# A one-core transformer layer with routed experts: the last three tiles' sums made on chip by TensorE, and the requests for rows moved in the transition

## The chip, the cores and the metric

The kernel runs on one core of one Trainium2 chip. The metric is device time in microseconds (us); lower is better. A core has five engines that run their own instruction queues and wait for each other by semaphores: TensorE (PE, with its weight loads PEld), VectorE (DVE), ScalarE (ACT), GpSimd (POOL) and SyncE (SP), which here only issues DMAs. POOL issues the indirect DMAs (scatter of rows, accumulation of rows in DRAM). All DMAs share 16 DMA engines.

## What is computed

```python
x = x + _layernorm(attention(_layernorm(x)))          # 4 x 256 tokens of 256, 16 heads of 128, rotary, causal
x = x + _layernorm(moe(_layernorm(x)))                # below
logits = x @ router_weight.T + router_bias            # 16 experts
top_val, top_idx = jax.lax.top_k(logits, 4)           # each token goes to 4 experts
gate_up = einsum('th,ehd->etd', x, gate_up_proj) + gate_up_proj_bias
glu = gate * sigmoid(1.702 * gate)                    # gate, up clipped at 7
out = einsum('etd,edh->eth', (up + 1.0) * glu, down_proj) + down_proj_bias
out = (out * router_scores.T[:, :, None]).sum(axis=0) # sum over a token's 4 experts
```

All data is float32.

## The kernel before

**Attention** runs over 64 slots (4 batches x 16 heads) and fills the first two thirds of the time. **Routing** follows batch by batch (`choose`, `share`, `place` on DVE; `ranks`, `counts` on PE): every token's normalised row, its expert weights and its token number (column TOKEN) are scattered by POOL to `rows_d` in DRAM, 4 times (once for each chosen expert), so that the rows of one expert stand together. 8 scatters belong to the last batch.

**The tiles.** The rows are then worked in TILE_MAX = 47 tiles of 128 rows, each of one expert. For tile i: SP loads its rows to `xg` (`load_rows`, 9 buffers; which rows, a table in SBUF says, and SP reads it first); PE turns them (`turn_tile`, into `xgT` by ACT), multiplies by the expert's weights, which DVE and ACT have copied to `gu_now` (`place_gu`, one half each; PE: `gate_up`); DVE clamps (`clamp`), ACT applies the gelu, DVE multiplies (`gated`); PE multiplies by the second weights (`down`); ACT scales by the router weight (`weigh`, to `y`); POOL adds the 128 rows of `y` to their tokens' rows in DRAM by an indirect DMA with addition (`add_rows`). There are SUMS = 3 arrays in DRAM, `sum0` to `sum2`, and tile i goes to array i % 3, so that additions to one array are never in flight together. `sum0` starts with the second bias term (`start_sum`, from `start_sums` on PE and `start_out` on ACT).

Tiles 0 to EARLY - 1 = 8 hold full tiles of the first three batches, known from `early_table` before the last batch is routed. They are worked while the last batch is routed; I call this stretch (about 331 to 380 us) the transition. Tiles 9 to 46 come from `table`, which needs all counts: PE `counts`, DVE `plan_tiles`, PE `table_rows`, DVE `table_out` (semaphore dve_table).

In the steady loop, PE's order in turn i is `turn_tile(i + 1)`, `gate_up(i)`, `down(i - 2)`; DVE's is `place_gu(i + 1)`, `clamp(i)`, `gated(i)`; ACT's is `place_gu(i + 1)`, `xgT_out(i + 1)`, `gelu(i)`, `weigh(i - 2)`. The order is written out by hand, for the transition call by call.

**The end.** When all additions have landed, SP loads the three arrays in 12 DMAs; for each quarter u (two of the eight groups of 128 tokens) DVE adds the three arrays and takes mean and variance, POOL computes 1/sqrt(var + eps) (`power`), ACT normalises, DVE adds `x`, and SP stores the quarter.

```python
for i in range(SUMS):
    sp.wait_ge(dma_sum[i], 16 * ((TILE_MAX - 1 - i) // SUMS + 1))
```

## Time and profile before

| | before |
|---|---|
| median of 3 runs | 517.08 us (516.77 to 518.73) |
| time of the profiled execution | 519.65 us |
| its span, first to last instruction | 517.8 us |
| busy: PE, PEld, DVE, ACT, POOL | 460.6, 430.1, 357.0, 327.3, 243.7 us |
| mean granted TensorE clock | 0.965 of full speed |

The span is what the trace shows; the profiled execution took 1.85 us more than its span. Busy shares are means over the whole kernel: PE is busy for 89% of the span, but not in the last 30 us. TensorE's clock is granted at one of two levels, 2.4 GHz (1.00) and 1.2 GHz (0.50).

### The profile page before, as it was taken

To read this page: it belongs to the slowest core of one execution; us is meant where nothing else is said; L and a number is where in the kernel's file an instruction comes from. 1 tells how busy PE (TensorE), PEld (TensorE's weight loads), DVE (VectorE), ACT (ScalarE), POOL (GpSimd) and SP (SyncE) were. 2 spreads that over 40 slices of the span, in tenths; PEclk is the share of its full clock that TensorE was granted. 3 is DMA by queue.
4 is the path that set the end of the run, shared out by engine and by line. 5 is a ranking of instruction groups with operands and counts; after the bars stand their busy time and mean duration, and the time that the engine had idled before them with its cause. 6 is when DMAs were issued, how large, how long until landed. Compare 5 with 4: busy or idle time off the path is not lost. (4 is left out here: it accounts for less than half of the span.)

```text
span 517.8 us, 11511 instructions
## 1 busy us (share of the span) xinstructions
PE 460.6 (89%) x3402; PEld 430.1 (83%) x3402; DVE 357.0 (69%) x1254; ACT 327.3 (63%) x815; POOL 243.7 (47%) x230
## 2 busy tenths in 40 slices
PE   7698999999999999999999999788799999999600
PEld 4698898999899999899999988677599999999500
DVE  4798787686865686865686896276557776767435
ACT  4778987767576767576767565555446565656602
POOL 1888874354122265343552145036625555555612
PEclk9999999999999999999999999898989999999955
DMA  7367552999300000000464455523545565655482
GB/s 238 108 204 245 179 184 66 373 369 370 112 1 1 22 25 35 35 13 35 174 219 123 151 199 186 161 61 90 107 92 97 100 103 95 102 95 87 52 243 92
DMA packets 63900, 67.86 MB, mean 131 GB/s; under 512 B 4640, under 2 KB 58720, under 8 KB 63840
## 3 DMA queue, kind: packets, MB, share of 16 engines
q1 hardware_dynamic: 54960, 55.79, 34.0%
q0 software_dynamic: 8304, 10.88, 12.8%
q8 instruction: 29, 0.48, 0.4%
q10 hardware_dynamic: 576, 0.46, 0.3%
q14 instruction: 31, 0.25, 0.2%
HBM read 32.63 MB, written 34.49 MB: 130 GB/s over the span
## 5 line engine op out<-in xcount | busy, mean ns | idle before, releaser
L494 POOL TENSOR_TENSOR by_sin<-by_sin,rope_sin 128x512 f32<-128x512 f32 x64 | 82.5, 1289 | 149.3 <-ACT by_sin L615 149.3
L590 POOL DMA_INDIRECT sum_d<-y,xg x47 | 72.9, 1551 | 64.5 <-ACT y L739 61.5
L615 ACT ACTIVATE by_sin<-bank 64x512 f32<-64x512 f32 x128 | 75.8, 592 | 33.9 <-PE bank L1246 32.5
L1444 PE MATMUL bank<-xgT,gu_now 128*128 128x128 f32 x752 | 94.0, 280 | 3.6 <-ACT xgT L615 2.7
L1444 PEld LDWEIGHTS bank<-xgT,gu_now 128*128 128x128 f32 x752 | 89.7, 196 | 4.6 <-issue 4.6
L637 ACT ACTIVATE prob<-score,row_bias 128x128 f32<-128x128 f32 (+1 forms) x128 | 57.1, 447 | 46.0 <-DVE row_bias L913 46.0
L1246 PE MATMUL bank<-xT_h,qk_h 128*128 128x256 f32 x256 | 77.6, 303 | 4.3 <-DVE qkT L903 1.7
L913 DVE CUSTOM_DVE_ANT_0 score<-bank,mask 128x128 f32<-128x128 f32 (+1 forms) x128 | 40.2, 351 | 52.1 <-issue 52.1
L1246 PE MATMUL bank<-xT_h,qk_l 128*128 128x256 f32 x256 | 72.3, 282 | 0.0
L1246 PE MATMUL bank<-xT_l,qk_h 128*128 128x256 f32 x256 | 72.2, 282 | 0.0
L1246 PEld LDWEIGHTS bank<-xT_h,qk_h 128*128 128x128 f32 x256 | 48.8, 191 | 5.1 <-POOL qk_l L479 3.4
L1456 PE MATMUL bank<-dn_w,act 128*128 x188 | 49.4, 388 | 1.1 <-DVE act L1111 1.0
L1246 PE MATMUL bank<-wo_h,oT_h 128*128 128x256 f32 x128 | 42.0, 328 | 9.3 <-DVE oT_l L928 9.1
L903 DVE TENSOR_TENSOR qkT<-bank,by_sin 128x512 f32<-128x512 f32 x64 | 44.2, 691 | 7.1 <-POOL by_sin L494 1.3
L1246 PEld LDWEIGHTS bank<-xT_l,qk_h 128*128 128x128 f32 x256 | 48.8, 191 | 0.0
L1246 PEld LDWEIGHTS bank<-xT_h,qk_l 128*128 128x128 f32 x256 | 48.7, 190 | 0.0
L1246 PE MATMUL bank<-wv_h,xT_h 128*128 128x256 f32 x128 | 47.5, 371 | 0.0
L895 DVE TENSOR_TENSOR bank<-bank,rope_cos 128x512 f32<-128x512 f32 x64 | 44.4, 694 | 1.2 <-ACT by_sin L615 1.2
L725 ACT ACTIVATE glu<-gate 128x256 f32<-128x256 f32 x47 | 19.6, 416 | 37.7 <-DVE gate L1095 37.7
L1095 DVE TENSOR_SCALAR gate<-bank,gate_bias 128x128 f32<-128x128 f32 x94 | 28.5, 345 | 20.6 <-PE bank L1444 20.4
L922 DVE TENSOR_SCALAR prob<-prob,row_rec 128x128 f32<-128x128 f32 (+1 forms) x128 | 40.3, 357 | 2.3
L615 ACT ACTIVATE gu_now<-gu_w 128x512 f32 x47 | 31.9, 678 | 15.8 <-issue 14.6
(171 smaller groups left out, 1141.0 us busy)
## 6 DMA issues: line engine op xcount, KB each, us to landing
rows_d<-blank SPq DMA_DIRECT2D x32, 576.0 KB, 7.4
gu_w<-_L_ffn_gate_up_proj_dram SPq DMA_DIRECT2D x16, 512.0 KB, 5.6
xg<-rows_d SPq DMA_DIRECT2D x47, 144.0 KB, 2.6
dn_w<-in_L_ffn_down_proj_dram SPq DMA_DIRECT2D x16, 256.0 KB, 3.0
sum_d<-blank SPq DMA_DIRECT2D x2, 1152.0 KB, 9.9
raw_qk<-in_L_attn_wq_dram SPq DMA_DIRECT2D x16, 128.0 KB, 3.6
raw_qk<-in_L_attn_wk_dram SPq DMA_DIRECT2D x16, 128.0 KB, 3.7
raw_v<-in_L_attn_wv_dram SPq DMA_DIRECT2D x8, 256.0 KB, 2.7
```

Of the source, the lines that this page charges most:

```text
L494: pool.tensor_tensor(v, v, rope_sin[:, :].unsqueeze(1).broadcast_to([P, 2, T]), ALU.mult).then_inc(pool_sin, 1)
L590: pool.indirect_dma_start(out=sum_d[i % SUMS], out_offset=bass.IndirectOffsetOnAxis(ap=xg[:, i % XG, TOKEN:TOKEN + 1].bitcast(U32), axis=0 ...
L615: return sc.activation(out, in_, ACT.Copy)
L637: e = sc.activation(prob[:, n % 2, lo:hi], score[:, n % 2, lo:hi], ACT.Exp, bias=row_bias[:, n % 2, i:i + 1], scale=-1.0, accum_out=row_su ...
L895: dve.tensor_tensor(v, v, rope_cos[:, :].unsqueeze(1).broadcast_to([P, 2, T]), ALU.mult).then_inc(dve_cos, 1)
L903: dve.tensor_tensor(qkT[:, n % QR, :, :].rearrange("p w t -> p (w t)"), ps_qk[n % 2][:, :], by_sin[:, n % 2, :], ALU.add).then_inc(dve_rop ...
L913: m = dve.tensor_tensor_reduce(score[:, n % 2, lo:hi], ps_s[:, lo:hi], mask[:, P:T] if i == 0 else mask[:, :], -1.0 / D, FILL, ALU.add, AL ...
L922: m = dve.tensor_scalar(prob[:, n % 2, lo:hi], prob[:, n % 2, lo:hi], row_rec[:, n % 2, i:i + 1], None, ALU.mult)
L1095: m = dve.tensor_scalar(gate[:, i % 2, r, :], ps_gu[i % 2][:, r * P:(r + 1) * P], gate_bias[:, bass.ds(e * 2 + r, 1)], LIMIT, ALU.add, ALU ...
L1246: m = pe.matmul(out, lhs, rhs, start=first and i == 0, stop=last and i == len(terms) - 1, skip_group_check=not (first and last))
L1444: m = pe.matmul(ps_gu[i % 2][:, (2 * s + r) * P:(2 * s + r + 1) * P], gu_now[:, i % 2, k, s, r * P:(r + 1) * P], xgT[:, i % XT, k, :], sta ...
L1456: m = pe.matmul(ps_y[i % 2][:, 0:M], act[:, i % AR, r, :], dn_w[:, bass.ds(e, 1), r, :].rearrange("p o m -> p (o m)"), start=(r == 0), sto ...
```

## The change

It has two parts, and small moves that go with them.

**The end.** The last LATE = 3 tiles (44 to 46) are no longer added in DRAM. ACT writes their weighted rows to `late_h` (rounded to the matmul's short float format) and DVE the rest to `late_l` (`late_low`). For each of these tiles DVE makes a 0/1 matrix `turn` (128 rows x 1024 tokens) from the token numbers (`rows_to_tokens`, in the turns of tiles 40, 41 and 42), and PE multiplies it with the rows, which puts them at their tokens (`add_late`, in PSUM). Since the arrays in DRAM are final after tile 43, SP loads them while the last tiles are worked: `sum2` after tile 41, `sum0` after 42, `sum1` after 43. POOL adds the three (`add_second`, `add_third`), and PE adds the result in PSUM by a product with the identity (`add_sums`). DVE takes the statistics from PSUM, `finish` multiplies and adds `x`, ACT adds the shift. `shift_x`, which ACT did at the end, goes into the turns of tiles 13 to 16.

**The transition.** SP asks for three tiles' rows before it stores the start of `sum0`; on PE, ACT and DVE several calls change place; POOL adds tile 2 after the 8 scatters instead of before.

```diff
@@ SP @@
-            start_sum(3)
             sp.wait_ge(dve_table, 1)
             sp.wait_ge(dma_scatter, 16 * TILES * TOP)
-            for i in range(EARLY, TILE_MAX):
+            for i in range(EARLY, EARLY + 3):
+                load_rows(i)
+            start_sum(3)
+            for i in range(EARLY + 3, TILE_MAX):
                 load_rows(i)
-
-            for i in range(SUMS):
-                sp.wait_ge(dma_sum[i], 16 * ((TILE_MAX - 1 - i) // SUMS + 1))
+            for i, to, signal in ((ENDING[0], sum_a, dma_first), (ENDING[1], sum_b, dma_second)):
+                sp.wait_ge(dma_sum[i], 16 * ((LAST - 1 - i) // SUMS + 1))
+                for u in range(2):
+                    sp.dma_start(to[:, 4 * u:4 * u + 4, :], sum_rows[i][:, 4 * u:4 * u + 4, :]).then_inc(signal[u], 16)
+            sp.wait_ge(dma_sum[ENDING[2]], 16 * ((LAST - 1 - ENDING[2]) // SUMS + 1))
             for u in range(4):
+                sp.dma_start(sum_c[:, 2 * u:2 * u + 2, :], sum_rows[ENDING[2]][:, 2 * u:2 * u + 2, :]).then_inc(dma_third[u], 16)
@@ POOL @@
-            for i in range(3):
+            for i in range(2):
                 add_rows(i)
             may_scatter(B - 1)
...
-            for i in range(EARLY, TILE_MAX):
+            for i in range(EARLY, LAST):
                 add_rows(i)
             for u in range(4):
+                add_second(u)
+            add_third(0)
+            add_third(1)
+            add_third(2)
+            power("moe", 0)
+            add_third(3)
@@ ACT @@
             gelu(1)
             normalise("b", B - 1, xn, x)
+            gelu(2)
+            moeT_out(B - 1)
             weigh(0, experts[0])
-            moeT_out(B - 1)
             weigh(1, experts[1])
-            gelu(2)
             gelu(3)
             load_table(ACT.Exp, 1)
             place_tile(4)
-            weigh(2, experts[2])
             expo_out(B - 1)
             load_table(ACT.Gelu_apprx_sigmoid, 2)
+            weigh(2, experts[2])
@@ DVE @@
             clamp(0, experts[0])
+            attn_stats(B - 1)
             experts[2] = place_gu(2)
-            attn_stats(B - 1)
...
             experts[7] = place_gu(7)
+            table_out()
             clamp(6, experts[6])
             gated(6)
             experts[8] = place_gu(8)
-            table_out()
...
+            def rows_to_tokens(j):
+                i = LAST + j
+                dve.wait_ge(dma_xg[i % XG], 16 * (i // XG + 1))
+                chain(dve.tensor_copy(token[:, j:j + 1], xg[:, i % XG, TOKEN:TOKEN + 1].bitcast(I32)))
+                chain(dve.tensor_scalar(from_end[:, j, :], full_edge[:, :], token[:, j:j + 1], None, ALU.subtract))
+                dve.tensor_tensor(turn[:, j, :, :], from_end[:, j, :].unsqueeze(2).broadcast_to([P, TILES, P]),
+                                  countdown[:, :].unsqueeze(1).broadcast_to([P, TILES, P]), ALU.is_equal).then_inc(dve_turn, 1)
             for i in range(EARLY, TILE_MAX):
...
                 gated(i)
+                if LAST - 4 <= i < LAST - 4 + LATE:
+                    rows_to_tokens(i - LAST + 4)
+            for j in range(LATE):
+                late_low(j, experts[LAST + j])
@@ PE @@
             down(2)
+            turn_tile(5)
             counts()
...
+            turn_tile(7)
             gate_up(6)
+            table_rows()
             down(5)
-            table_rows()
             start_sums(B - 1)
-            turn_tile(7)
+            turn_tile(8)
             gate_up(7)
...
+            def add_late(u, j, first=False, last=False):
+                pe.wait_ge(dve_turn, j + 1)
+                pe.wait_ge(dve_late, j + 1)
+                for s in range(2):
+                    for rows in (late_h, late_l):
+                        m = pe.matmul(ps_sum[u][:, s * M:(s + 1) * M], turn[:, j, 2 * u + s, :], rows[:, j, :], ...)
+            def add_sums(u):
+                pe.wait_ge(pool_whole, u + 1)
+                for s in range(2):
+                    pe.matmul(ps_sum[u][:, s * M:(s + 1) * M], ident[:, :], sum_a[:, 2 * u + s, :], start=False, stop=False, ...)
+            for u in range(4):
+                add_late(u, 0, first=True)
+            for u in range(4):
+                add_late(u, 1)
+                add_sums(u)
+                add_late(u, 2, last=True).then_inc(pe_sum, 1)
```

On SP, behind the last early tile's load, there stood (L376 stores the start of `sum0`, `started`; L428 reads the table, L431 loads rows):

```order
L431 DMA xg<-rows_d 128x288
L376 DMA sum_d<-started 128x2x256 [waits act_start]
L428 TENSOR_LOAD table [waits dma_scatter,dve_table]
L428 ISA x2
L431 ISA [waits dma_sum0]
```

Now the same queue goes on without the store (L393 there), which comes three loads later:

```order
L448 DMA xg<-rows_d 128x288
L445 TENSOR_LOAD table [waits dma_scatter,dve_table]
L445 ISA x2
L448 ISA [waits dma_sum0]
L448 DMA xg<-rows_d 128x288
L445 TENSOR_LOAD table
L445 ISA x2
L448 ISA [waits dma_sum1]
L448 DMA xg<-rows_d 128x288
L445 TENSOR_LOAD table
L445 ISA x2
L448 ISA [waits dma_sum2]
```

So the first request for tile 9's rows no longer stands behind a wait for ACT's `start_out` (act_start).

On PE, around `gate_up(6)` of the transition, there stood (L1444 `gate_up`, L1456 `down`, L1422 `table_rows`, L1411 `start_sums`, L1431 `turn_tile`):

```order
L1444 MATMUL bank<-xgT,gu_now 128x128 x7
L1451 TENSOR_LOAD early_table
L1451 ISA x2
L1456 ISA [waits act_y,dve_act]
L1456 MATMUL bank<-dn_w,act 128x256
L1456 ISA
L1456 MATMUL bank<-dn_w,act 128x256
L1422 MATMUL bank<-ident,plan 1x128 [waits dve_plan]
L1422 MATMUL bank<-ident,plan 1x128
L1411 MATMUL bank<-dnb,routeT 128x256 [waits act_routeT]
L1411 MATMUL bank<-dnb,routeT 128x256
L1431 MATMUL bank<-ident,xg 128x128 [waits act_xgT,dma_xg7]
```

Now there stands (L1509 `turn_tile`, L1522 `gate_up`, L1500 `table_rows`, L1536 `down`):

```order
L1509 MATMUL bank<-ident,xg 128x128 [waits act_xgT,dma_xg7]
L1509 MATMUL bank<-ident,xg 128x128
L1522 MATMUL bank<-xgT,gu_now 128x128 [waits act_xgT,dve_up,act_gu,dve_gu]
L1522 MATMUL bank<-xgT,gu_now 128x128 x7
L1500 MATMUL bank<-ident,plan 1x128 [waits dve_plan]
L1500 MATMUL bank<-ident,plan 1x128
L1529 TENSOR_LOAD early_table
L1529 ISA x2
L1536 ISA [waits act_y,dve_act]
L1536 MATMUL bank<-dn_w,act 128x256
```

The turn of tile 7 stands ahead of `gate_up(6)` instead of right before `gate_up(7)`, so that ACT can copy it while PE multiplies; tiles 5, 6 and 8 move in the same way. `table_rows` stands ahead of `down(5)`.

On DVE, in the turns of tiles 40, 41 and 42, three rows are new behind `gated` (L1169), ahead of the next `place_gu` (L1140, L1143):

```order
L1169 SCALAR_TENSOR_TENSOR act<-up,glu 128x256 [waits pe_y,dve_up,act_glu]
L1277 CAST token<-xg 128x1 [waits dma_xg8]
L1278 TENSOR_SCALAR from_end<-full_edge,token 128x8 [waits dve_stat]
L1279 TENSOR_TENSOR turn<-from_end,countdown 128x1024 [waits dve_stat]
L1140 TENSOR_LOAD table
L1140 ISA x2
L1143 ISA [waits pe_gu]
L1143 COPY gu_now<-gu_w 128x512
```

Before, `place_gu` followed at once. PE's next `gate_up` waits for that copy (dve_gu).

## Rows read from the trace of the kernel before

**Rows 1.** The chain that ended last, in order of time: start, us, what

```profile
490.58 3.74 DMA sum_d<-y,xg
...
495.32 4.16 DMA sum_c<-sum_d
...
506.82 0.75 DVE stats L876 x2
...
510.08 0.75 DVE stats L876 x2
...
511.16 0.17 DVE var_eps L883
...
513.21 0.85 DVE sum_b L1226 x2
```

**Rows 2.** Busy time in stretches of the end: PE, PEld, DVE, ACT, POOL, clock, DMA

```profile
488.00:494.00 6.00, 0.08 (x1) 0.00 (x0) 0.00 (x0) 3.66 (x9) 3.52 (x3) 0.83 0.57 66
500.00:505.00 5.00, 0.00 (x0) 0.00 (x0) 4.79 (x17) 1.09 (x2) 1.41 (x3) 0.50 1.05 345
```

**Rows 3.** Timeline of the transition: start, us, engine, line, instruction, idle before

```profile
348.37 0.18 DVE L966 TENSOR_TENSOR logits<-bank,rb 128x32 f32<-128x32 f32 x1
...
362.84 0.96 POOL L497 DMA_INDIRECT rows_d<-xrow,slot_of  x1 [0.30 <-issue]
...
367.71 0.40 DVE L1065 CAST table<-bank 1x256 int32<-1x256 f32 x1
...
371.78 5.50 SPq L431 DMA_DIRECT2D xg<-rows_d  x5
...
376.18 0.69 PE L1431 MATMUL bank<-ident,xg 128*128 128x128 f32 x2 [1.78 <-DMA xg<-rows_d]
...
379.94 1.95 PE L1444 MATMUL bank<-xgT,gu_now 128*128 128x128 f32 x16
```

**Rows 4.** Time from issue to landing of the last batch's eight scatters

```profile
DMA to landing us min/median/max: 2.4/2.5/3.5
```

**Rows 5.** Busy time in one stretch of the transition, columns as in rows 2

```profile
375.90:379.30 3.40, 3.12 (x15) 3.12 (x16) 0.34 (x1) 0.38 (x1) 0.00 (x0) 0.50 0.83 176
```

**Rows 6.** Timeline of the steady loop, one turn, in part

```profile
475.88 0.43 DVE L1085 COPY gu_now<-gu_w 128x512 f32 x1 [0.34 <-issue]
476.78 0.61 DVE L1095 TENSOR_SCALAR gate<-bank,gate_bias 128x128 f32<-128x128 f32 x2 [0.46 <-PE bank L1444]
477.42 0.42 ACT L725 ACTIVATE glu<-gate 128x256 f32<-128x256 f32 x1 [0.72 <-DVE gate L1095]
477.55 0.72 PE L1444 MATMUL bank<-xgT,gu_now 128*128 128x128 f32 x5
```

**Rows 7.** Groups by form: busy us, mean ns of one, idle before

```profile
L494 POOL TENSOR_TENSOR by_sin<-by_sin,rope_sin 128x512 f32<-128x512 f32 x64 | 82.5, 1289 | 149.3 <-ACT by_sin L615 149.3
L903 DVE TENSOR_TENSOR qkT<-bank,by_sin 128x512 f32<-128x512 f32 x64 | 44.2, 691 | 7.1 <-POOL by_sin L494 1.3 <-issue 0.4
L928 DVE TENSOR_TENSOR oT_l<-bank,oT_h 128x256 fp32r<-128x256 f32 x64 | 27.2, 425 | 18.9 <-ACT oT_h L615 18.8
L1074 DVE TENSOR_TENSOR wv_l<-raw_v,wv_h 128x512 fp32r<-128x512 f32 x1 | 1.8, 1791 | 0.0
```

**Rows 8.** Timeline of PE: pace of short-format products and of float32 products

```profile
204.22 0.28 PE L1246 MATMUL bank<-wo_h,oT_h 128*128 128x256 f32 x1
204.34 0.28 PE L1246 MATMUL bank<-wo_l,oT_h 128*128 128x256 f32 x1
...
353.57 1.49 PE L1456 MATMUL bank<-dn_w,act 128*128 x3
```

**Rows 9.** Additions in DRAM near the end: issues on POOL, and their time to landing

```profile
478.47 1.55 POOL L590 DMA_INDIRECT sum_d<-y,xg  x1 [1.32 <-ACT y L739]
...
484.40 1.56 POOL L590 DMA_INDIRECT sum_d<-y,xg  x1 [1.50 <-ACT y L739]
...
DMA to landing us min/median/max: 3.6/3.8/4.8
```

More of the change, by code:

```diff
@@ L41 @@
 BLANK = E * REGION
-XG, XT, AR, YR, SUMS = 9, 2, 3, 5, 3
+XG, XT, AR, YR, SUMS, LATE = 9, 2, 3, 5, 3, 3
 FILL_STEP = 4
@@ L175, in block_kernel @@
         sum_c = sb("sum_c", [P, TILES, M])
+        turn = sb("turn", [P, LATE, TILES, P], F32R)
+        late_h = sb("late_h", [P, LATE, M], F32R)
+        late_l = sb("late_l", [P, LATE, M], F32R)
+        token = sb("token", [P, LATE])
+        from_end = sb("from_end", [P, LATE, TILES])
         rows_d = nc.dram_tensor("rows_d", (BLANK + P, ROW), F32).ap()
@@ L214, in block_kernel @@
         dma_sum = [sem(f"dma_sum{i}") for i in range(SUMS)]
-        dma_result = [sem(f"dma_result{u}") for u in range(4)]
+        dma_first = [sem(f"dma_first{u}") for u in range(2)]
+        dma_second = [sem(f"dma_second{u}") for u in range(2)]
+        dma_third = [sem(f"dma_third{u}") for u in range(4)]
+        dve_turn = sem("dve_turn")
+        dve_late = sem("dve_late")
+        pool_first = sem("pool_first")
+        pool_whole = sem("pool_whole")
+        pe_sum = sem("pe_sum")
         dma_out = sem("dma_out")
@@ L329, in v_split @@
                 eng.wait_ge(pool_v, g + 1 - DVE_PAIRS)
+        LAST = TILE_MAX - LATE
+        ENDING = [(LAST + k) % SUMS for k in range(SUMS)]
         def entry(i, column):
@@ L602, in _, with add_second, add_third @@
                     scatter(t, k)
-            for i in range(3, EARLY):
+            for i in range(2, EARLY):
                 add_rows(i)
             pool.wait_ge(dma_start, 16 * B)
-            for i in range(EARLY, TILE_MAX):
+            for i in range(EARLY, LAST):
                 add_rows(i)
-            for u in range(4):
+            def add_second(u):
+                pool.wait_ge(dma_first[u // 2], 16)
+                pool.wait_ge(dma_second[u // 2], 16)
+                tiles = slice(2 * u, 2 * u + 2)
+                pool.tensor_tensor(sum_a[:, tiles, :], sum_a[:, tiles, :], sum_b[:, tiles, :], ALU.add).then_inc(pool_first, 1)
+            def add_third(u):
+                pool.wait_ge(dma_third[u], 16)
+                pool.wait_ge(pool_first, u + 1)
+                tiles = slice(2 * u, 2 * u + 2)
+                pool.tensor_tensor(sum_a[:, tiles, :], sum_a[:, tiles, :], sum_c[:, tiles, :], ALU.add).then_inc(pool_whole, 1)
+            for u in range(4):
+                add_second(u)
[4 more added lines that the diff above has]
+            add_third(3)
+            for u in range(1, 4):
                 power("moe", u)
@@ L736, in weigh @@
                 sc.wait_ge(pe_y, i + 1)
+                if i >= LAST:
+                    sc.activation(late_h[:, i - LAST, :], ps_y[i % 2][:, 0:M], ACT.Copy,
+                                  scale=xg[:, i % XG, bass.ds(e + M, 1)]).then_inc(act_y, 1)
+                    return
                 if i >= YR:
@@ L852, in _, with shift_result @@
                     weigh(i - 2, experts[i - 2])
+                if EARLY + 4 <= i < EARLY + 8:
+                    shift_x(i - EARLY - 4)
+            def shift_result(u):
+                n = NORMS.index(("moe", u))
+                sc.wait_ge(pool_shift, n + 1)
+                sc.wait_ge(dve_out, u + 1)
+                for i in range(2):
+                    sc.activation(sum_b[:, 2 * u + i, :], sum_b[:, 2 * u + i, :], ACT.Identity,
+                                  bias=shift[:, 2 * n + i:2 * n + i + 1]).then_inc(act_moe, 1)
             for u in range(4):
-                shift_x(u)
-            for u in range(4):
-                normalise("moe", u, sum_a, sum_a, act_moe)
+                shift_result(u)
         @block.vector
@@ L1454, in down @@
                     pe.wait_ge(act_y, i - 1)
+                if i - 2 >= LAST:
+                    pe.wait_ge(dve_late, i - 1 - LAST)
                 for r in range(2):
@@ L1558, in _ @@
                     down(i - 2)
+            def add_late(u, j, first=False, last=False):
[3 more added lines that the diff above has]
+                    for rows in (late_h, late_l):
+                        m = pe.matmul(ps_sum[u][:, s * M:(s + 1) * M], turn[:, j, 2 * u + s, :], rows[:, j, :],
+                                      start=first and s == 0 and rows is late_h, stop=last and s == 1 and rows is late_l,
+                                      skip_group_check=True)
+                return m
+            def add_sums(u):
+                pe.wait_ge(pool_whole, u + 1)
+                for s in range(2):
+                    pe.matmul(ps_sum[u][:, s * M:(s + 1) * M], ident[:, :], sum_a[:, 2 * u + s, :], start=False, stop=False,
+                              skip_group_check=True)
+            pe.wait_ge(act_xgT, TILE_MAX)
+            for u in range(4):
[4 more added lines that the diff above has]
+                add_late(u, 2, last=True).then_inc(pe_sum, 1)
 _INS = ["L0_attn_x", "L0_attn_wq", "L0_attn_wk", "L0_attn_wv", "L0_attn_wo", "L0_ffn_router_weight", "L0_ffn_router_bias",
```

44 lines of the change are left out of this document (24 added, 20 removed).

## The prediction

> **What bounds the kernel now.** I read the chain that ended last first, since it says where an earlier step gives an earlier end. From 490.58 us on it holds no PE work at all: the last addition in DRAM (3.74 us), the loads of the three arrays (the first DVE step of the end waits for a DMA issued at 495.32 that takes 4.16 us), then DVE, quarter by quarter, and the last store [rows 1]. Two quarters' statistics start at 506.82 and 510.08, so a quarter costs DVE 3.26 us; the last var_eps ends at 511.33, and DVE's last instruction at 514.06, with 3.7 us of store behind it to the end of the span, 517.8. Next the busy time in stretches: from 488 to 494 PE does nothing, and the clock is already at its lower level for part of it; from 500 to 505 it is 0.50 and the DMA engines are full at 345 GB/s [rows 2]. So the end is bound by DMA latency and then by DVE. Ahead of it the steady loop is PE's: one tile each 2.87 us (additions at 478.47 and 484.40, two tiles apart less one late start of 0.2 [rows 9]), with DVE idle 0.46 us and ACT 0.72 us in each turn [rows 6]. In the transition PE is starved: tile 10's turn at 376.18 waited 1.78 us for rows that SP began to ask for at 371.78 (tile 9's), though the last scatter was issued at 362.84 and the table stood at 368.11 [rows 3]. And gate_up(9), which follows it, ran in a stretch at clock 0.50 [rows 5].
>
> **Term 1, the transition: -6.0.** SP's first request needs the table and the landed scatters. The scatters: ACT's gelu(2) now comes before the wait for moeT, so DVE's clamp(3) is done earlier and choose starts when the logits are there, about 0.9 us sooner than 348.37 [rows 3]; with weigh(2) out of expo's way about 1.1 us at the scatters. The last is issued at 361.7 instead of 362.84 and lands 2.5 us after [rows 4], 364.2. The table: before, DVE waited in turn 4 for a gelu that stood on ACT behind the turn of tile 5, and that turn stood on PE behind down(3). With the turns moved ahead, plan_tiles ends about 2.7 us sooner, at 358.2; table_rows then stands right behind gate_up(6) and table_out ahead of clamp(6), which puts the table at about 361 instead of 368.11. So the scatters decide, SP's first request goes out near 365.3 (a table read of 1.1 us behind it) instead of 371.78. Five requests took 5.50 us [rows 3], one each 1.29, so tile 10's was issued at 373.07 and its rows ended PE's wait at 376.18: 3.1 us. Tile 9's rows are there at about 368.4. PE walks its six tiles 4 to 9 almost without waits then: I place gate_up(4) to (9) at 350.0, 354.0, 357.2, 362.3, 365.2, 370.1, and gate_up(10) at 372.4 against 379.94, a gain of 7.5. Hand-placed starts leave out small gaps and a stretch at the lower clock like the one in rows 5 that may come elsewhere (1.5 us). I take 6.0. Bounds: 3.1 (the wait of 1.78 us and the 1.3 us that gate_up(9) lost at half clock go, 3.28 from its start to gate_up(10)'s instead of 1.95; nothing else) and 7.5. What could be late next: tile 11's request waits for tile 2's addition, now issued behind the eight scatters, near 362.9, landed by 367 at 3.8 us [rows 9]; its rows are wanted at 372.5, so 3 us of cover.
>
> **Term 2, the loop: +3.2.** rows_to_tokens puts three instructions in front of a copy that PE waits for. Two DVE element-wise forms fix the price of the third: 425 ns for 256 columns, 691 for 512 [rows 7], hence 1.04 ns a column and 1.22 us for 1024. The two small ones with their waits take some 0.2 each (I take DVE's short chained instructions, 0.15 to 0.17 us plus 0.05). 1.67 us in each of three turns, 5.0 in all. What hides them: the copy now ends at 476.31, and the gate_up that needs it starts at 477.55 [rows 6], 1.24 us; and DVE's idle 0.46 in the second and third turn [rows 6]. 5.0 - 1.24 - 0.92 = 2.85 us that PE loses for good, for PE is the bound and never catches up. Bounds: 1.8 (if the table reads, 0.34 us of idle a turn [rows 6], hide behind the new instructions), and the rival below. shift_x: two ACT instructions in each of four turns, at 0.42 as the gelu of the same size [rows 6] 0.84 together, against 0.72 idle in a turn [rows 6] and some slack of xgT: 0.1 to 0.5, I take 0.3.
>
> **Term 3, the end: -4.1.** In the old clock, with the delay of term 2 left out. Additions of tiles 41, 42, 43 are issued at 478.5, 481.3, 484.4 and land 3.8 us on [rows 9]. sum2's 1 MB is asked for at 482.3, sum0's near 485.5, sum1's near 489; each takes 3 us at 345 GB/s [rows 2], and the additions in flight share the engines with them, so I put tile 43's landing 0.8 later than alone and the first two arrays complete at 491. POOL's sums are 1.29 us each [rows 7], 1.32 with the gap: four add_second from 489.6 end at 494.9, the first add_third at 496.2. sum1's quarters are there from 492 on and don't hold it. So POOL's queue bounds PE's first add_sums, at 496.3. PE's work for a quarter: two add_late at 4 products each of 0.12 us (starts at 204.22 and 204.34 [rows 8]), 0.96; add_sums is two float32 products of 256 columns in 4 pieces, like a down. At the lower clock three pieces of a down took 1.49 us [rows 8]; with 0.63 for the last, they stood 0.43 apart, so add_sums takes 1.7 there and half, 0.86, at the full clock. A quarter is 1.82 us at the full clock and, with the short products' 0.96 nearly doubled to 1.8, 3.5 us at the lower. Which clock? PE's twenty early products (add_late of tile 44, and of 45 for quarter 0) end near 491, then PE waits 5.3 us; before, it stopped at 488.1 and the clock was down within 4 us [rows 2]. So the first quarter runs at 0.50. After the dip of rows 5, in which PE was busy, the clock was full again after 3.4 us; so I take quarter 0 and most of quarter 1 slow, the rest full: 496.3 + 3.5 + 2.6 + 1.8 + 1.8 = 506.0, less 0.5 for products of tile 45 already done: 505.5. Behind it: statistics 1.35 (510.08 to 511.33 [rows 1], and the hand-over), POOL's power 0.9, two multiply-adds, a little over the two last additions' 0.85 [rows 1] since they read PSUM, 0.98, ACT's two 1.15: 509.9 against 514.06. Bounds: 503.5 if the clock stays up (then POOL's power ahead of its last sum holds quarter 3), so -6.4; and 496.3 + 14.0 - 0.5 = 509.8, end 514.2, so 0, if it stays down. late_low(0) ahead of down(46) delays PE by 0.4 us; it is hidden by the wait for POOL.
>
> On the clock the rows stand alone above. TensorE: Matmul & The Clock Gate of the Trainium skill (What's actually happening; Wait — 56ns, not 53.3ns?) says that idleness brings the array to 1.2 GHz and activity back to 2.4, and that a product then takes N/1.2 instead of N/2.4 ns plus 2.5. For 256 columns that is 213 against 109 ns; the trace agrees with its pitch of 120 ns at the full clock [rows 8]. By the page's figures the eight short products of a quarter would take 1.7 us at the low clock, and term 3 would be 0.2 us better.
>
> **Sum.** -6.0 + 2.9 + 0.3 - 4.1 = -6.9 on the profiled execution's own 519.65 (span 517.8), 512.75. The median of the runs shown is 2.57 below that execution, so 517.08 - 6.9 = **510.2**.
>
> **Rivals.** (a) *The tail stays at the low clock* (term 3 is 0): 514.3. For: nothing in the trace shows PE work of this kind there, and the clock is 0.50 from 492 to the end. Against: the dip of rows 5 ended with PE busy in it. (b) *The 0/1 matrices wait for POOL.* The DVE forms with two SBUF operands had one case of 1791 ns for 512 columns beside POOL's work [rows 7], where 691 is usual; turn's matrix has two SBUF operands, and POOL issues an addition (1.55 us [rows 9]) in just that part of each turn. If each matrix first waits for that, term 2 grows by 4.65: 514.8. Against: copies that stand beside POOL's issues take their usual 0.43 [rows 6]. SBUF — State Buffer of the Trainium skill (Terms: shared port pair) says DVE and GpSimd lock a shared port pair for a whole instruction and that the loser blocks fully. (c) *Slower: (b) at its full price.* If the matrix both waits 1.55 and runs at 1791 ns per 512 columns, a turn's addition is 1.55 + 3.58 + 0.45 = 5.6, three make 16.7, less 2.15 of cover 14.6 instead of 2.85: 521.9. The sum turns to slower once a matrix costs over 3.5 us with its wait (6.9 / 3 + 1.22), and by over 0.5% from 4.4 us. (d) *The transition's moves give only the bound of 3.1*, because the PE order starves elsewhere: 513.1; or nothing at all, since the scatters and not the table hold SP: 516.2. For: the scatters move by 1.1 only; against: they landed 6 us before the request went out.
>
> **Chances.** Forecast with its bounds (506.5 to 513.5) 0.66; (a) 0.11; (b) 0.08; (c) 0.04; (d) weak 0.08, nothing 0.03. 0.5% is 2.6 us, about what a measurement of this kernel can tell from no change: faster means below 514.5, slower above 519.7. Faster: the forecast, nearly all of weak (d), half of (a) and a third of (b): 0.82. Same: the others' rest, 0.13. Slower: (c) and mixtures, 0.05. The range, 505.5 to 514.8, leaves out (c), the empty (d) and a little at both ends.
>
> **What would show it.** SP's first request for tile 9's rows near 365, gate_up(10) near 374, no PE wait for rows there; gate_up of tiles 41 to 43 delayed by 2.9 in all, DVE's 1024-column instruction at 1.22 us; add_sums(0) about 10 us behind down(46), after a wait for POOL, at clock 0.50; quarters 1.8 to 3.5 us apart instead of 3.26. The prediction is wrong if SP's request still waits (for tile additions or the scatters), if the matrix takes over 3.5 us with its wait, or if the loads beside the additions end after 496 and hold POOL's last sums.

## The result and the profile after

The changed kernel takes 512.56 us, the median of 4 runs (509.63 to 516.86), beside 517.57 for the kernel before on the same chip (4 runs): a ratio of 0.9882, 95% interval 0.9834 to 0.993. Repeated on two other chips it was 0.9876 (0.9811 to 0.9941) and 0.9892 (0.9841 to 0.9943). A ratio leaves out the runs that took over 1.5% longer than the fastest of the same kernel, which on the chip called B below are 8 of the 13 runs of the kernel before and none of the four kernels beside it. The forecast of 510.2 was 2.4 us too low; the range and the sign hold. Of the 2.4 us, 0.5 lies in the start (517.57 by four runs, where the forecast began at 517.08) and 1.9 in the gain, 5.0 us by the medians where 6.9 was said. The profiled execution took 514.36 with a span of 512.6, against 519.65 and 517.8: 5.3 us, where the sum said 6.9.

The transition, on PE (columns as in rows 3; L1522 is gate_up, L1536 down, L1509 a tile's turn; the three shown first of L1522 are those of tiles 4, 7 and 9, and the last line is tile 10's, of which the view shows ten pieces of sixteen):

```profile
350.06 3.56 PE L1522 MATMUL bank<-xgT,gu_now 128*128 128x128 f32 x16
...
361.26 1.13 PE L1536 MATMUL bank<-dn_w,act 128*128 x4 [1.16 <-DVE act L1169]
...
363.78 3.45 PE L1522 MATMUL bank<-xgT,gu_now 128*128 128x128 f32 x16
...
370.58 0.60 PE L1509 MATMUL bank<-ident,xg 128*128 128x128 f32 x4
372.91 2.02 PE L1522 MATMUL bank<-xgT,gu_now 128*128 128x128 f32 x16 [1.73 <-ACT xgT L659]
...
374.99 1.28 PE L1522 MATMUL bank<-xgT,gu_now 128*128 128x128 f32 x10
```

Tile 10's products start at 374.99 where they started at 379.94 [rows 3]. No wait for rows is left on PE here (on chip D, below, 0.64 us of one is); what is left is a wait for ScalarE's copy of tile 9 and two tiles (4 and 7) at nearly twice the 1.95 us of the full clock. Choose started at 347.42, and the queues beside it show the last scatter (L517) and SyncE's first request (L448):

```profile
361.36 0.96 POOL L517 DMA_INDIRECT rows_d<-xrow,slot_of  x1 [0.30 <-issue]
...
364.66 3.31 SPq L448 DMA_DIRECT2D xg<-rows_d  x3
```

The request came 7.1 us sooner than before (371.78 [rows 3]). In the loop, DVE in the first turn that makes a matrix (L1169 is gated, L1277 to L1279 make the matrix, L1143 is the copy for the next tile, L1153 the clamp), then parts of turns without one; and PE's gate_up of the last tiles:

```profile
464.43 0.43 DVE L1169 SCALAR_TENSOR_TENSOR act<-up,glu 128x256 f32<-128x256 f32 x1
464.81 0.15 DVE L1277 CAST token<-xg 128x1 f32<-128x1 int32 x1
465.00 0.23 DVE L1278 TENSOR_SCALAR from_end<-full_edge,token 128x8 f32<-128x8 f32 x1
465.27 1.23 DVE L1279 TENSOR_TENSOR turn<-from_end,countdown 128x1024 fp32r<-128x1024 f32 x1
466.41 0.42 DVE L1143 COPY gu_now<-gu_w 128x512 f32 x1
...
474.92 0.43 DVE L1169 SCALAR_TENSOR_TENSOR act<-up,glu 128x256 f32<-128x256 f32 x1
475.69 0.43 DVE L1143 COPY gu_now<-gu_w 128x512 f32 x1 [0.35 <-issue]
...
478.06 0.43 DVE L1143 COPY gu_now<-gu_w 128x512 f32 x1 [0.37 <-issue]
478.92 0.61 DVE L1153 TENSOR_SCALAR gate<-bank,gate_bias 128x128 f32<-128x128 f32 x2 [0.43 <-PE bank L1522]
```

```profile
466.88 2.05 PE L1522 MATMUL bank<-xgT,gu_now 128*128 128x128 f32 x16
470.37 2.05 PE L1522 MATMUL bank<-xgT,gu_now 128*128 128x128 f32 x16 [0.35 <-DVE gu_now L1143]
473.85 2.05 PE L1522 MATMUL bank<-xgT,gu_now 128*128 128x128 f32 x16 [0.34 <-DVE gu_now L1143]
476.82 1.95 PE L1522 MATMUL bank<-xgT,gu_now 128*128 128x128 f32 x16
479.47 1.95 PE L1522 MATMUL bank<-xgT,gu_now 128*128 128x128 f32 x16
```

DVE has no idle time in the turn with a matrix, and PE's gate_up follow each other after 3.49 us where it was 2.87, in two turns. The last tile's gate_up (tile 46) starts at 479.47; before it was 483.07. The end, on GpSimd and SyncE, then on PE (L1655 is add_sums) and DVE (L934, the first statistics):

```profile
480.80 1.57 POOL L612 DMA_INDIRECT sum_d<-y,xg  x1 [1.51 <-ACT y L787]
487.73 1.90 SPq L476 DMA_DIRECT2D sum_c<-sum_d  x4
489.02 4.91 POOL L636 TENSOR_TENSOR sum_a<-sum_a,sum_b 128x512 f32<-128x512 f32 x4 [6.65 <-DMA sum_b<-sum_d]
493.89 3.70 POOL L643 TENSOR_TENSOR sum_a<-sum_a,sum_c 128x512 f32<-128x512 f32 x3
495.20 2.07 PE L1655 MATMUL bank<-sum_a,ident 128*128 128x256 f32 x4 [7.82 <-POOL sum_a L643]
...
498.17 0.76 DVE L934 BATCH_NORM_STATS2 stats<-bank 128x6 f32<-128x256 f32 x2 [11.93 <-PE bank L1646]
```

Of the chain that ended last, these pieces lie ahead of GpSimd's first sum (columns as in rows 1):

```profile
477.75 4.32 DMA sum_d<-y,xg
482.08 6.80 DMA sum_b<-sum_d
489.02 1.36 POOL sum_a L636 x2
```

So GpSimd's sums wait for the first half of the second array (`sum0`, loaded to `sum_b`), which landed 6.8 us after its request. Tile 43's addition is issued at 480.80; the load of the third array, which waits for it, goes out at 487.73, 6.9 us later, where an addition took 3.8 [rows 9]. That lateness holds nothing here: GpSimd's additions of the third array (L643) follow the others without a wait. The busy time in stretches of the end (columns as in rows 2) answers to rows 2:

```profile
489.00:500.00 11.00, 4.80 (x15) 4.23 (x16) 1.22 (x6) 0.00 (x0) 9.08 (x8) 0.54 0.30 95
500.00:510.00 10.00, 4.53 (x30) 4.03 (x28) 6.77 (x26) 3.62 (x8) 4.31 (x9) 0.84 0.24 82
```

### The profile page after: what moved, and what is told of

Same layout as the page of the kernel before. It is cut to its first block and busy times, and to the rows that moved or that the text cites. A ratio compares the mean times of both kernels' runs of the same rounds, so it can differ in the third digit from the quotient of the medians.

```text
span 512.6 us, 11665 instructions
## 1 busy us (share of the span) xinstructions
PE 469.9 (92%) x3466; PEld 439.8 (86%) x3466; DVE 356.6 (70%) x1258; ACT 325.5 (63%) x815; POOL 248.5 (48%) x236
## 5 line engine op out<-in xcount | busy, mean ns | idle before, releaser
L1522 PE MATMUL bank<-xgT,gu_now 128*128 128x128 f32 x752 | 95.1, 281 | 3.6 <-ACT xgT L659 1.7
L612 POOL DMA_INDIRECT sum_d<-y,xg x44 | 68.5, 1558 | 58.7 <-ACT y L787 55.1
L1522 PEld LDWEIGHTS bank<-xgT,gu_now 128*128 128x128 f32 x752 | 90.9, 198 | 5.0 <-DVE gu_now L1143 3.8
L1536 PE MATMUL bank<-dn_w,act 128*128 x188 | 48.4, 382 | 1.9 <-DVE act L1169 1.2
L1153 DVE TENSOR_SCALAR gate<-bank,gate_bias 128x128 f32<-128x128 f32 x94 | 28.5, 345 | 20.7 <-PE bank L1522 20.6
```

The lines of the kernel that those rows point to most:

```text
L612: pool.indirect_dma_start(out=sum_d[i % SUMS], out_offset=bass.IndirectOffsetOnAxis(ap=xg[:, i % XG, TOKEN:TOKEN + 1].bitcast(U32), axis=0 ...
L1153: m = dve.tensor_scalar(gate[:, i % 2, r, :], ps_gu[i % 2][:, r * P:(r + 1) * P], gate_bias[:, bass.ds(e * 2 + r, 1)], LIMIT, ALU.add, ALU ...
L1522: m = pe.matmul(ps_gu[i % 2][:, (2 * s + r) * P:(2 * s + r + 1) * P], gu_now[:, i % 2, k, s, r * P:(r + 1) * P], xgT[:, i % XT, k, :], sta ...
L1536: m = pe.matmul(ps_y[i % 2][:, 0:M], act[:, i % AR, r, :], dn_w[:, bass.ds(e, 1), r, :].rearrange("p o m -> p (o m)"), start=(r == 0), sto ...
```

## The experiments

All times of a kernel depend on the chip that it ran on, so ratios are to the kernel before on the same chip. Four chips were used: A for the result above, B, C and D. Since runs of one kernel spread over 7 us (509.86 to 517.39 for after_third), I read three stretches from PE's own rows, in us: T from the first gate_up of tile 0 to that of tile 10, L from there to tile 46's, E from there to the end of the span. They are differences of starts in each profiled execution, one for each kernel: where the end is the changed kernel's own, E alone goes from 31.8 to 33.2.

| kernel | chip | ratio (95%) | T | L | E |
|---|---|---|---|---|---|
| before | A | | 45.80 | 103.13 | 34.75 |
| after | A | 0.988 (0.983 to 0.993) | 41.19 | 104.48 | 33.08 |
| before_again | D | 1.001 (0.998 to 1.004) | 45.48 | 103.13 | 35.70 |
| after_third | D | 0.989 (0.984 to 0.994) | 41.66 | 104.48 | 31.80 |
| sp_back | D | 0.986 (0.980 to 0.991) | 41.69 | 104.91 | 32.55 |
| four_edits | D | 0.976 (0.972 to 0.979) | 38.60 | 103.14 | 28.97 |
| transition_only | B | 0.984 (0.978 to 0.990) | 46.48 | 103.13 | 35.48 |
| end_only | B | 1.005 (1.001 to 1.010) | 49.26 | 104.49 | 33.17 |
| busy_wait | B | 0.976 (0.971 to 0.982) | 44.71 | 104.49 | 30.88 |
| loads_last | B | 0.987 (0.982 to 0.993) | 46.38 | 104.49 | 35.72 |
| after_again | C | 0.988 (0.981 to 0.994) | 46.01 | 104.77 | 32.67 |
| dve_sums | C | 0.988 (0.981 to 0.996) | 46.47 | 104.48 | 29.57 |
| tile9_sooner | C | 0.984 (0.977 to 0.991) | 45.15 | 104.55 | 32.38 |
| matrix_split | C | 0.983 (0.976 to 0.990) | 45.05 | 103.13 | 31.80 |

### The two halves of the change apart (chip B)

*transition_only*: the kernel before, with the new orders on the five engines and SyncE's sooner requests, and the old end.

```diff
 PE:    down(2)  +turn_tile(5)  counts() ranks(B-1) gate_up(4) down(3)
        +turn_route(B-1) +turn_tile(6) gate_up(5) ... gate_up(6) +table_rows() down(5)
 SyncE: -start_sum(3)  wait table, scatters  load_rows 9..11  +start_sum(3)  load_rows 12..
```

> The kernel before with only the moves of the transition (order of calls on PE, ACT, DVE, POOL's tile 2 behind the scatters, SP's three requests before the store of sum0's start); the end stays as before. Theory A, the gains of the two parts add: in the changed kernel gate_up(10) stood at 374.99 us instead of 379.94, so this kernel is 5.0 us faster than before, 512.5 against 517.5, and its steady loop stands 5.0 us earlier. Rival B, the gain is eaten behind the transition (the loop is held by additions or row requests): gate_up(10) is early but the last gate_up is less than 4 us early. Rival C: the clock decides, the stretches at 0.50 fall elsewhere and the gain differs by 1.5 us or more.

*end_only*: the changed kernel with these orders put back; the matrices and the new end stay.

```diff
 PE:    -turn_tile(5) after down(2)   -table_rows() ahead of down(5)
 SyncE: +start_sum(3) ahead of the wait for table and scatters
```

> The changed kernel with the transition put back as it was before; only the end is new. Theory A: the matrices cost the loop 1.35 us and the end gives 1.6 back with this clock, so 517.3 against 517.5, no change; with a clock that stays up at the end up to 3 us faster. Rival B, the end is worth what was forecast (4.1 less 2.9): 516.3, not to be told from A by time, but by the trace: the last gate_up 2.9 late instead of 1.35. Rival C: without the transition's gain the end loses, over 519.

Measured: 0.984 and 1.005. By the stretches each half has its own: T is 49.26 with the old orders and 44.7 to 46.5 with the new (three kernels on B), so the orders give 2.8 to 4.6 us. L is 103.13 without the matrices and 104.49 with them. E is 35.48 and 33.17, 2.3 us. So the matrices and the new end alone are worth 2.3 - 1.36 = 0.95 us by these stretches. The ratio puts end_only 0.1 to 1.0% above the kernel before instead, but it compares all ten runs of end_only with the five fastest of the thirteen of the kernel before; by the medians of all runs end_only is 1.6 us faster (528.05 beside 529.61), which agrees with the stretches. No trace of the kernel before was taken on B, and the trace of end_only is of its fastest run (524.13), that of transition_only of its slowest (523.95), so these differences are good to a few us only. The transition carries the larger part of the result: on A 4.6 us of T against 0.3 for the matrices and the end together, on D (below) 3.8 against 2.55.

### The clock in the end (chip B)

*busy_wait*: the changed kernel, and 28 products of the identity with itself, into a bank that nobody reads, ahead of the first add_sums.

```diff
                 add_late(u, 1)
+                if u == 0:
+                    pe.wait_ge(dve_up, TILE_MAX)
+                    keep_busy(ident[:, :], ident[:, :], 28, bank[2])
                 add_sums(u)
```

> The changed kernel, with 28 float32 products of the identity with itself (128 columns, 0.244 us each at the full clock, 6.8 us in all) on PE in a free PSUM bank while it waits for POOL's first whole sum. They add work and change no result. Theory A, the lower clock in the end costs: the clock stays at 1.00 through add_sums, each quarter takes PE 1.8 us instead of 2.1 to 3.6, the end comes 1.5 to 2.5 us earlier than in the profile of the changed kernel, and the spread between executions (509.6 to 516.9) shrinks. Rival B: POOL and DVE hold the quarters anyway and the end moves by less than 0.7 us. Rival C: the products delay the first add_sums, and the time grows.

Measured 0.976. Its rows on PE; L1495 are the added products:

```profile
493.76 6.41 PE L1495 MATMUL bank<-ident 128*128 128x128 f32 x56
501.23 1.13 PE L1655 MATMUL bank<-sum_a,ident 128*128 128x256 f32 x4 [1.06 <-POOL sum_a L643]
```

An add_sums group is recorded with 1.13 us instead of 2.08, the clock from 500 to 510 us reads 1.00 (0.51 in end_only), the first statistics come 1.64 us behind add_sums instead of 2.97, and E is 30.88 against 33.17 of end_only, which has the same end: 2.3 us for a wait filled with idle work. That is against one execution in which two groups ran slow (2.08 and 1.91 us). From the first add_sums to the end of the span busy_wait takes 15.7 us, end_only 17.9 and the other executions in which GpSimd makes these sums 17.0 to 17.6, so the clock's price is 1.3 to 2.2. The changed kernel unaltered was not run on B, so the time of busy_wait has no partner there.

### The landing beside the loads (chip B)

*loads_last*: the loads of the first two arrays also wait for tile 43's addition.

```diff
+            sp.wait_ge(dma_sum[ENDING[2]], 16 * ((LAST - 1 - ENDING[2]) // SUMS + 1))
             for i, to, signal in ((ENDING[0], sum_a, dma_first), (ENDING[1], sum_b, dma_second)):
```

> The changed kernel, with all loads of the three DRAM sums asked for only when tile 43's addition has landed (8 DMAs, 3 MB). In the changed kernel that addition took 6.9 us to land beside the loads and the two before it 4.3 to 4.6. Theory A, contention: without loads beside it the addition lands in 3.8 to 4.3 us, that is 2.7 us earlier, but 3 MB then need 9 us, so the last quarter of sum1 is there near 494 to 495 instead of 493 and POOL's first sum starts about 1 us later: net 1 to 2 us slower than the changed kernel. Rival B: the addition is slow for another reason and lands in 6.9 again: the end is 4 us or more later. Rival C: no difference, since POOL's seven sums bind.

```profile
486.32 1.57 POOL L612 DMA_INDIRECT sum_d<-y,xg  x1 [1.51 <-ACT y L787]
490.21 0.94 SPq L474 DMA_DIRECT2D sum_a<-sum_d  x2
...
497.53 4.92 POOL L636 TENSOR_TENSOR sum_a<-sum_a,sum_b 128x512 f32<-128x512 f32 x4 [9.63 <-DMA sum_b<-sum_d]
```

The addition lands 3.9 us after its issue when alone, against 6.9 (A), 7.8 and 8.2 (B) and 7.9 (C) beside the loads: the collision is shown and delays the landing by 3 to 4.3 us. But E is 35.72: the arrays now come late (the first sum on GpSimd starts 12.5 us behind tile 46's gate_up, 9.0 and 9.1 in the other two kernels with the new end on B), and the overlap is worth more than the collision costs.

### Unaltered on chip C, and three edits

*after_again*: the changed kernel.

> The changed kernel unaltered, as the measure for the three kernels that run beside it. Its loop from the tenth tile's gate/up products to the last tile's should again be 1.3 to 1.4 us longer than the loop before the change, and the stretch from the last tile's products to the end of the span 33 us. If the second chip's extra time is in the chip and not in the kernels, the transition shows it here too: a copy of the table on VectorE that waits 8 us.

E is 32.67 and L 104.77. T is 46.01, 4.8 longer than on A; the last section shows what lies in it.

*matrix_split*: each 0/1 matrix in two halves of 512 columns, in six turns.

```diff
-                if LAST - 4 <= i < LAST - 4 + LATE:
-                    rows_to_tokens(i - LAST + 4)
+                if LAST - 4 <= i < LAST - 4 + 2 * LATE:
+                    rows_to_tokens((i - LAST + 4) // 2, (i - LAST + 4) % 2)
```

> Each 0/1 matrix is made in two halves, in six turns of the loop in place of three. Theory 1 (the loop loses time because a turn with a whole matrix asks more of VectorE than a turn of TensorE lasts, 3.49 against 2.87 us): with half a matrix a turn fits, and the 1.35 us come back but for 0.3 at most. Theory 2 (any operation more on VectorE in these turns delays the next tile's copy of the weights): the six shorter operations cost as much as the three, 1.35 us or more, and the time does not fall.

```profile
471.76 0.43 DVE L1169 SCALAR_TENSOR_TENSOR act<-up,glu 128x256 f32<-128x256 f32 x1
472.11 0.68 DVE L1281 TENSOR_TENSOR turn<-from_end,countdown 128x512 fp32r<-128x512 f32 x1
472.71 0.42 DVE L1143 COPY gu_now<-gu_w 128x512 f32 x1
```

L is 103.13, the figure of the kernels without any matrix: the work is as long, in turns that have room for it, and costs nothing. Theory 1 holds.

*dve_sums*: the eight additions of the loaded arrays on DVE instead of GpSimd.

```diff
-                pool.tensor_tensor(sum_a[:, tiles, :], sum_a[:, tiles, :], sum_b[:, tiles, :], ALU.add).then_inc(pool_first, 1)
+                dve.tensor_tensor(sum_a[:, tiles, :], sum_a[:, tiles, :], sum_b[:, tiles, :], ALU.add).then_inc(pool_first, 1)
```

> The eight additions of the loaded arrays are moved from GpSimd to VectorE, which stood idle for 11.9 us there. Theory 1 (the additions at 1.22 to 1.29 us each are on the path after the arrays have landed): VectorE takes 0.6 to 0.7 us for one, the first add_sums starts 2 to 3 us sooner after the last landing, and the time falls by 2 to 3 us. Theory 2 (the landing of the third array decides): add_sums(0) moves by under 1 us, the later quarters by nothing, and the time falls by under 1 us.

```profile
496.84 2.51 DVE L1283 TENSOR_TENSOR sum_a<-sum_a,sum_b 128x512 f32<-128x512 f32 x4 [2.62 <-DMA sum_b<-sum_d]
499.42 1.39 DVE L1290 TENSOR_TENSOR sum_a<-sum_a,sum_c 128x512 f32<-128x512 f32 x2
500.17 2.08 PE L1653 MATMUL bank<-sum_a,ident 128*128 128x256 f32 x4 [4.80 <-DVE sum_a L1290]
501.39 1.36 DVE L1290 TENSOR_TENSOR sum_a<-sum_a,sum_c 128x512 f32<-128x512 f32 x2 [0.58 <-DMA sum_c<-sum_d]
```

Four sums take 2.51 us instead of 4.91, the first add_sums comes 12.7 us behind tile 46's gate_up instead of 15.7, and E falls from 32.67 to 29.57, 3.1 us: theory 1. Behind it the third array's landing is the next bound (0.58). The medians do not show it (519.37 beside 519.11): the profiled execution reached tile 0 at 336.50, against 333.33, with the clock at 0.56 from 81 to 84 us and at 0.63 and 0.52 between 330 and 334, where after_again has 1.00, ahead of all that the edit touches; whether the other runs did too, their totals don't tell.

*tile9_sooner*: turn_tile(9) ahead of down(7) on PE, and tile 9's two weight copies ahead of tile 8's work.

```diff
             gate_up(8)
+            pe.wait_ge(dve_table, 1)
+            turn_tile(EARLY)
             down(7)
-
-            pe.wait_ge(dve_table, 1)
-            turn_tile(EARLY)
```

> The turn of tile 9 stands ahead of the down products of tile 7, and both copies of its weights stand ahead of tile 8's work on ScalarE and VectorE. Theory 1 (what kept the transition from giving the 6.0 us is the order in which tile 9 is taken up once its rows have landed): the 1.7 to 1.8 us that its products waited go, and the time falls by 1.5 to 2. Theory 2 (the rows of the tiles behind it bound the transition): the wait comes back at tile 10, 11 or 12 as a wait for a landing, and the time stays within 0.5 us.

PE's wait ahead of tile 9's products, 1.57 us in after_again, is gone: from tile 8's gate_up to tile 9's it is 4.91 us instead of 6.42, with tile 8's at the lower clock in both (3.62 and 3.54), and no wait for rows comes in its place at tile 10. T is 45.15, only 0.86 under after_again, because VectorE's wait for the table was 0.7 us longer (7.87 against 7.17; see the last section). So the trace shows theory 1's 1.5 us. The time does not: matrix_split, whose transition is unaltered, has a T of 45.05, since its tile 8 ran only in part at the lower clock (2.51 instead of 3.54), and the median of tile9_sooner is 1.8 us lower than that of after_again, within the intervals.

### The request alone, before on another chip, and all edits (chip D)

*after_third* and *before_again* are the two kernels unaltered.

> The changed kernel unaltered once more, as the measure for the three beside it. From the last tile's gate/up products to the first add_sums 15.7 us, to the end of the span 32.7 to 33.1. If this chip has the stretch in which TensorE completes nothing for 7 to 8 us (seen on two chips, not on the first), the copy of the table on VectorE waits that long.

> The kernel before the change, for its trace on a chip other than the first. If TensorE's halt in the transition belongs to the chip, it is here too, at the same place in the program (around the products with the weights of tile 6), and the stretch from the fourth tile to the tenth is some 3.5 us longer than on the first chip (32.4 against 29.0 us). If it belongs to the new order alone, it is absent and the stretch takes 29.0.

On D neither has a halt of PE: T is 45.48 and 41.66, as on A. The change gives 3.8 us in T, costs 1.35 in L and gives 3.9 in E, in sum 6.4, less 0.8 because tile 0 starts later here (334.91, 334.07): 5.5 in the spans, 518.4 and 512.8. Of the 3.9 in E, 0.95 is that the old end took longer here than on A.

*sp_back*: SyncE's start_sum(3) ahead of the three requests again.

```diff
+            start_sum(3)
             sp.wait_ge(dve_table, 1)
             sp.wait_ge(dma_scatter, 16 * TILES * TOP)
-            for i in range(EARLY, EARLY + 3):
-                load_rows(i)
-            start_sum(3)
-            for i in range(EARLY + 3, TILE_MAX):
+            for i in range(EARLY, TILE_MAX):
                 load_rows(i)
```

> SyncE's start of the last quarter of the sums stands ahead of the three requests for rows again; all else as changed. Theory 1 (the sooner request is a part of the transition's gain by itself): the requests wait for the copy of the quarter on ScalarE and come 1 to 3 us later, and so do the products of tiles 9 and 10 and the end. Theory 2 (the gain comes from the engines' orders; on the first chip the copy came at 365.45 and the first request at 364.66): the requests come under 1.2 us later, the products of tile 10 move by under 0.5, and the time stays.

```profile
365.49 0.38 SPq L393 DMA_DIRECT2D sum_d<-started  x1
366.72 8.96 SPq L448 DMA_DIRECT2D xg<-rows_d  x7
```

```profile
371.82 0.44 PE L1507 MATMUL bank<-ident,xg 128*128 128x128 f32 x2 [1.67 <-DMA xg<-rows_d]
```

The first request goes out at 366.72 against 366.07 in after_third, but the last scatter was issued 1.36 us sooner here (361.27 and 362.63): behind it the request came after 5.45 us instead of 3.44. So the store of `start_sum(3)` costs the request 2.0 us, and PE waits 1.67 us for tile 10's rows (the second line) where it waited 0.64 in after_third. That is theory 1's first half. Its second is not seen: T is the same (41.69 and 41.66), and so is the time (the median of its other three runs, without one of 1196 us, is 512.65; after_third has 513.98). But the two executions ran different tiles at the lower clock (4, 9 and in part 10 here; 7 and 9 in after_third), which is worth some 3 us in either, so what the 2.0 us are worth in the end is not settled. Most of the 7.1 us on A is due to table and scatters all the same: with the store ahead of the requests the first still went out 5.0 us sooner than in before_again (371.70).

*four_edits*: matrix_split, dve_sums and tile9_sooner together, and

```diff
+                    keep_busy(ident[:, :], ident[:, :], 20, bank[2])
                 add_sums(u)
```

> The matrices in halves, the eight additions on VectorE, tile 9 taken up sooner, and 20 products to keep TensorE busy ahead of the first add_sums, together. If the terms add: 1.4 for the halves, 3.0 for the additions, 0.9 to 1.5 for tile 9, 1.3 to 1.7 for the clock, so 6.6 to 7.6 us less than the changed kernel. If the landing of the third array takes over as the bound behind the additions, the clock's part shows but the additions give no more than 3.0; if the clock's dips elsewhere decide, the sum is hidden in the spread of the runs, and only the stretches from tile to tile show it.

Measured: 506.80 (504.42 to 508.22), ratio 0.9756 (0.9719 to 0.9793), faster than both kernels: 7.2 us under after_third. The spans differ by 7.9: T 3.1, L 1.34, E 2.8, and 0.6 by the start of tile 0. In E the edits do not add up (3.1 and 2.3 would be 5.4), for the statistics of the first quarter stand on DVE behind the last sums, which wait for the third array:

```profile
491.24 1.36 DVE L1292 TENSOR_TENSOR sum_a<-sum_a,sum_c 128x512 f32<-128x512 f32 x2 [1.11 <-DMA sum_c<-sum_d]
491.29 1.03 PE L1654 MATMUL bank<-sum_a,ident 128*128 128x256 f32 x4
492.51 0.76 DVE L912 BATCH_NORM_STATS2 stats<-bank 128x6 f32<-128x256 f32 x2
```

The 3.1 us of T match the clock's part: after_third ran two gate_up at 3.38 and 3.57 us, four_edits none (1.95, 1.96), which is 3.0 us. The clock over 358 to 366 and 366 to 380 was 0.80 and 0.87 in after_third; in four_edits it reads 1.00 in both:

```profile
358.00:366.00 8.00, 6.89 (x47) 5.55 (x47) 5.76 (x19) 4.71 (x11) 6.28 (x6) 1.00 0.32 98
366.00:380.00 14.00, 12.01 (x93) 10.87 (x92) 8.51 (x26) 6.98 (x16) 8.63 (x6) 1.00 0.88 159
```

Which of the edits kept it up, or whether it was chance, stays open; no kernel had this part's edit alone on this chip.

## Why the prediction held, point by point

- **Term 1, -6.0: the mechanism right, the size too large by about 1 us on A and 2 on D.** The request came at 364.66 (365.3 was said), choose 0.95 sooner (0.9), no wait for rows. Tile 10 started 4.95 us sooner on A. The hand-placed start of 372.4 was missed by 2.6: 0.75 by tile 5, since gate_up(4) ran at the lower clock (0.3 of it came back by tile 6); 1.05 at gate_up(7), with down(5)'s wait of 1.16 for DVE; 1.25 more by tile 8, since gate_up(7) too ran at about 0.5. The working had 1.5 us for the clock in all. four_edits, at the full clock, started tile 10 at 372.87, so the placing was about right (that kernel takes up tile 9 in another order) and the allowance for the clock short. Of the sooner request, moving it past the store gave 2.0 us (sp_back); whether PE's products gained by that part is not settled.
- **Term 2, +3.2: too large by 1.85.** On A, D and B the loop grew by 1.35 to 1.36 us (two of the kernels with whole matrices, sp_back and after_again, have 0.3 to 0.4 more). The matrix was priced right (1.22, measured 1.23). What the three instructions add to a turn was not: from gated to the copy DVE takes 1.98 us with them (464.43 to 466.41) and 0.77 without (474.92 to 475.69), so 1.21 where the sum had 1.67. The table read, 0.34 a turn, hides behind the matrix, which the working kept as a bound, and the small two are a little shorter. The cover was a little larger too: from the copy's start to the clamp's it is 0.86 us in a plain turn (478.06 to 478.92), with a wait for PE in it, and 0.34 in the turn with a matrix, so 0.52 is saved in each of two turns. 3 x 1.21 - 1.24 - 2 x 0.52 = 1.35, below the working's own bound of 1.8. shift_x, put at 0.3, cost nothing: L of transition_only, without it, is that of matrix_split, with it.
- **Term 3, -4.1: too large on two chips of three.** Measured by E: -1.7 (A), -2.3 (B), -3.9 (D). The first add_sums was to come 13.2 us behind tile 46's gate_up and came 15.7 behind on A, 14.8 on D. The step that failed is "four add_second from 489.6", 6.5 us behind that gate_up: they started 9.55 behind it, 3.0 later, and GpSimd's sums, 1.23 us each where 1.29 was taken, gave 0.5 back. What held them is the first half of the second array, with 6.8 us from request to landing where the working left 4.1. The price of 3 us for each 1 MB was that of loads with the DMA engines to themselves; the first array's loads (asked for at 479.22, three us ahead) and tile 43's addition were still in flight (no run tells their shares apart). Tile 43's landing, put 0.8 later than alone, was 3 to 4.3 later, but in the changed kernel no sum waits for it; in dve_sums, where the sums are quicker, one does (0.58). The clock was judged rightly: 0.54 from 489 to 500, back in the second quarter, so that statistics stand 2.8, 2.0 and 2.2 us apart. Its price in the bounds is 2.3 us (-6.4 against -4.1; the ends given with them, 503.5 and 505.5, make it 2.0), and busy_wait measured 1.3 to 2.2.
- The misses partly cancel, which is luck: on A the sum said 1.05 and 2.4 too much of gain and 1.85 too much of loss, 1.6 us in all, which is 6.9 against the 5.3 by which the spans differ.
- **Rivals.** (b) and (c) fell: the matrices took 1.23 us beside GpSimd's additions (the first, 465.27 to 466.50, beside one of 464.91 to 466.46). What the Trainium skill's page SBUF — State Buffer (Terms: shared port pair) says, that the loser of DVE and GpSimd blocks fully, is not seen here; GpSimd's instruction in these turns issues a DMA. (a) fell, the clock came back. (d), a transition worth 3.1 only, fell on A with 4.95; on D the 3.8 of T lie between it and the forecast.
- GPSIMD Engine Reference of the Trainium skill (3.1 Elementwise — side-by-side cycle accounting) has an element of a two-input addition at about 2.6 cycles on GpSimd and 1 on DVE, and 1.96 times the duration measured for 2048 columns. Here 512 columns took 1.23 and 0.63 us in a row of four (4.91 and 2.51), a factor of 1.96 as well.

## What to carry to other kernels

Work added to an engine that is not the bound costs what exceeds a turn's room, instruction reads included: count the idle time of every turn it can spread into, then cut it to fit (1.36 us became 0). Price a DMA that stands beside bulk loads, or a load that stands beside others, by a row that has such loads beside it, not by its time alone. When a chain ends in waits, ask which idle engine could do the last steps (3.1 us) and whether the tensor engine is at its lower clock when they end (1.3 to 2.2 us).

## What the runs showed of the hardware

On chips B and C, in all eight profiled executions there, PE's results came late in the transition, as if it had halted; on A and D, in six, they did not. In after_again, PE's products for the table, and then those of tile 7 with gaps:

```profile
357.40 0.60 PE L1500 MATMUL bank<-ident,plan 128*1 128x128 f32 x4
...
361.50 0.72 PE L1522 MATMUL bank<-xgT,gu_now 128*128 128x128 f32 x5
362.53 0.27 PE L1522 MATMUL bank<-xgT,gu_now 128*128 128x128 f32 x1 [0.32 <-issue]
363.24 1.08 PE L1522 MATMUL bank<-xgT,gu_now 128*128 128x128 f32 x4 [0.44 <-issue]
```

```profile
366.87 0.41 DVE L1123 CAST table<-bank 1x256 int32<-1x256 f32 x1 [7.17 <-remote]
```

DVE's copy of the table waits 7.2 us (6.8 to 8.1 in the other kernels with the new order; in end_only, with the old one, waits of 3.8 on DVE and 5.0 on ScalarE stand near the same place) for products that PE took up at 357.40. DVE and ScalarE wait alike and go on together, which points at PE's array itself; no run separates that from a late signal. The clock in after_again read 1.00 until 363 us and 0.50 from 364. T is 3 to 5 us longer on these chips, with either order; the cause is open. The second surprise is the spread: the clock falls in other places from run to run, and each fall in a stretch that PE bounds costs about 1.5 us (3.45 instead of 1.95 for a gate_up), which is as much as a term of this sum.
